# A graph-attention kernel: the scatter's one-hot made by ScalarE from a table of places instead of turned by TensorE, with a third PSUM bank for the expansion

## The reference, cut to what matters

```python
def _L0_gnn_ref(triplet_h, src, dst, Wqkv, bqkv, ...):
    h = layernorm(triplet_h, ln_attn_g, ln_attn_b)
    qkv = (h @ Wqkv + bqkv).reshape(n, 3, H, DH)
    q, k, v = qkv[:, 0] * SCALE, qkv[:, 1], qkv[:, 2]
    scores = jnp.einsum('ehd,ehd->eh', q[src], k[dst])
    m = jax.ops.segment_max(scores, dst, num_segments=n)
    e = jnp.exp(scores - m[dst])
    s = jax.ops.segment_sum(e, dst, num_segments=n)
    he = (v[src] * (e / s[dst])[:, :, None]).reshape(-1, D)
    agg = jax.ops.segment_sum(he, dst, num_segments=n)
    x = triplet_h + agg
    ...
```

## Time and profile before

| | us |
|---|---|
| median of 3 runs (3794.98 to 3800.59) | 3797.36 |
| span of the profiled execution, first to last instruction | 3773.2 |
| PE busy of it | 2896.0 (77%) |
| DVE busy | 2133.7 (57%) |
| POOL busy | 1732.1 (46%) |
| ACT busy | 963.3 (26%) |

### The profile page before, as it was taken

One profiled execution on the slowest core, in us unless ns is written; L12 is line 12 of the kernel. 1 busy time (PEld: TensorE's weight loads), 2 busy tenths in 40 slices (PEclk: granted clock), 3 DMA queues, 4 the chain that ended last, 5 costly groups with the idle time before them and its releaser, 6 DMA issues. The chain is left out here.

```text
span 3773.2 us, 52431 instructions
## 1 busy us (share of the span) xinstructions
PE 2896.0 (77%) x13207; PEld 1940.5 (51%) x13207; DVE 2133.7 (57%) x4604; ACT 963.3 (26%) x2525; POOL 1732.1 (46%) x1863
## 2 busy tenths in 40 slices
PE   6838888888888888869999999992655555555555
PEld 4525555555555555549998888871333333333332
DVE  6727776677767777768862222222544444444446
ACT  3513333333333333346663333330000000000000
POOL 2555655555555555433300000006466666666661
PEclk9968998899989999979999999995867677776678
DMA  4455666666666666533345444445233333333332
GB/s 151 147 166 164 196 192 193 181 192 189 194 188 190 192 191 195 160 114 99 99 136 210 187 186 188 187 178 164 69 91 92 92 92 92 91 91 92 92 92 88
DMA packets 233908, 557.07 MB, mean 148 GB/s; under 512 B 48498, under 2 KB 128454, under 8 KB 221095
## 3 DMA queue, kind: packets, MB, share of 16 engines
q0 software_dynamic: 104144, 324.24, 30.4%
q1 hardware_dynamic: 108463, 193.61, 14.1%
q10 hardware_dynamic: 21032, 35.85, 3.2%
HBM read 402.87 MB, written 150.71 MB: 147 GB/s over the span
## 5 line engine op out<-in xcount | busy, mean ns | idle before, releaser
L1294 POOL DMA_INDIRECT rel_rows<-msg_d,msg_i_again x783 | 743.3, 949 | 976.8 <-ACTq L1274 571.7
L1314 PE MATMUL rel_ps<-rel_rows,rel_hot 128*128 x1664 | 678.5, 538 | 525.0 <-issue 364.4
L873 POOL DMA_INDIRECT qv_rows<-qv_d,src_i x832 | 798.4, 960 | 567.6 <-PE out_ps L1155 354.2
L1314 PEld LDWEIGHTS rel_ps<-rel_rows,rel_hot 128*128 128x128 f32 x1664 | 367.1, 254 | 836.5 <-issue 806.3
L1339 DVE TENSOR_TENSOR sums_all<-sums_all,rel_ps 128x256 f32 x832 | 350.4, 421 | 630.4 <-PE rel_ps L1314 247.0
L1155 PE MATMUL out_ps<-qv_rows,hot 128*128 128x264 f32 x1664 | 635.8, 467 | 44.8 <-DVE qv_rows L950 25.0
L1031 ACT COPY at_acc<-out_ps 128x264 f32 x832 | 310.3, 380 | 726.9 <-PE out_ps L1155 581.1
L1110 PE MATMUL kx<-k,hot_t 128*128 x2496 | 398.4, 297 | 64.4 <-issue 48.4
L896 DVE TENSOR_TENSOR qv_rows<-qv_rows,kx 128x512 f32<-128x512 f32 x416 | 278.7, 679 | 204.4 <-remote 121.6
L1957 PE MATMUL up_hid_ps<-up_split,ms_hTs 128*128 128x512 f32 x1416 | 347.5, 396 | 0.0
L1110 PEld LDWEIGHTS kx<-k,hot_t 128*128 128x128 bf16 x2496 | 252.9, 105 | 175.4 <-issue 108.6
(11 more groups left out here) (213 smaller groups left out, 2883.3 us busy)
## 6 DMA issues: line engine op xcount, KB each, us to landing
msg_d<-up_x SPq DMA_DIRECT2D x33, 1024.0 KB, 3.9
msg_d<-up_gelu SPq DMA_DIRECT2D x33, 1024.0 KB, 3.8
msg_d<-up_res SPq DMA_DIRECT2D x32, 1024.0 KB, 3.8
dl_b<-dlt_d ACTq DMA_DIRECT2D x50, 512.0 KB
qv_rows<-qv_d,src_i POOLq DMA_INDIRECT x832
rel_rows<-msg_d,msg_i_again POOLq DMA_INDIRECT x783
qv_d<-qv SPq DMA_DIRECT2D x6, 1820.0 KB, 7.2
agg_d<-at_acc SPq DMA_DIRECT2D x49, 132.0 KB
```

Source lines behind the costliest of these rows:

```text
L873: nc.gpsimd.indirect_dma_start(rows[:, n % SLOTS, :], None, qv_d, bass.IndirectOffsetOnAxis(ap=src_i[:, n:n + 1], axis=0)).then_inc(got[n ...
L1294: nc.gpsimd.indirect_dma_start(rows[:, at:at + FEAT], None, table, bass.IndirectOffsetOnAxis(ap=msg_i[:, e:e + 1], axis=0)).then_inc(got[e ...
L1314: nc.tensor.matmul(sum_ps[n % BANKS][:], hot[:, n % HOTS, :], rows[:, bass.ds(at, FEAT)], start=True, stop=True).then_inc(summed, 1)
```

## The change

ACT makes `hot` itself. For each step it writes |place - number| over a row of the numbers 0 to 127 (`iota_n`) into a bf16 buffer `away`, with the place of each partition's edge as a per-partition bias; for each quad it then writes relu(1 - away) into `hot`. The places come from `late_d[0]`, loaded once into `dloc` by SP ahead of the first `dl_b`. `turn_hot`, `hot_ps` and the semaphore `turned` are gone. The freed bank is a third one for `kx`, and `hot_t` has two buffers for three. The 16 new instructions per round stand singly between ACT's old ones, except for the second quad's four, which stand together, and the copy of step 15 moves ahead of them.

```diff
-HOT_RING = 3
+HOT_RING = 2
+KX_RING = 3
...
+        away = sb(ctx, "at_away", [P, 2, QUAD, P], BF16)
-        kx = [ps(ctx, f"kx{i}", [P, BATCH, FEAT]) for i in range(2)]
-        hot_ps = ps(ctx, "hot_ps", [P, QUAD, P], BF16)
+        dloc = sb(ctx, "at_dloc_s", [P, STEPS])
+        kx = [ps(ctx, f"kx{i}", [P, BATCH, FEAT]) for i in range(KX_RING)]
...
     def on_sync(sp):
         sp.sem_inc(stored, 1)
+        sp.dma_start(dloc[:], late_d[0]).then_inc(dloc_ld, 16)
...
             if k >= HOT_RING:
-                dve.wait_ge(turned, QUADS * (k - HOT_RING + 1))
+                dve.wait_ge(kx_ok, BATCHES * (k - HOT_RING + 1))
...
-        def turned_back(k, i):
-            act.wait_ge(turned, QUADS * k + i + 1)
+        def away_from(k, i, q):
+            n = UNROLL * k + QUAD * i + q
+            last = nc.scalar.activation(away[:, i % 2, q, :], iota_n[:], ACT.Abs, scale=-1.0, bias=dloc[:, n:n + 1])
+            if q == QUAD - 1:
+                last.then_inc(away_ok, 1)
+
+        def one_hot(k, i):
+            act.wait_ge(away_ok, QUADS * k + i + 1)
             if k >= 1:
                 act.wait_ge(summed, UNROLL * (k - 1) + QUAD * (i + 1))
-            nc.scalar.copy(hot[:, QUAD * i:QUAD * (i + 1), :], hot_ps[:]).then_inc(hotf_ok, 1)
+            nc.scalar.activation(hot[:, QUAD * i:QUAD * (i + 1), :], away[:, i % 2], ACT.Relu, scale=-1.0, bias=1.0).then_inc(hotf_ok, 1)
...
             if now:
+                away_from(k - 1, 0, 0)
+                away_from(k - 1, 0, 1)
                 row_ends(k - 1)
...
                 evacuate(k - 2, banks, UNROLL - 4)
+            if now:
+                away_from(k - 1, 0, 2)
+            if before:
                 evacuate(k - 2, banks, UNROLL - 3)
             if now:
+                away_from(k - 1, 0, 3)
                 columns(k - 1)
...
             if now:
-                turned_back(k - 1, 0)
+                one_hot(k - 1, 0)
...
+            if before:
+                evacuate(k - 2, banks, UNROLL - 1)
             if now:
-                turned_back(k - 1, 1)
+                for q in range(QUAD):
+                    away_from(k - 1, 1, q)
+                one_hot(k - 1, 1)
             if further:
                 load_breaks(act, k + 1)
-            if before:
-                evacuate(k - 2, banks, UNROLL - 1)
...
                 evacuate(k - 1, banks, 0)
+                away_from(k - 1, 2, 0)
                 evacuate(k - 1, banks, 1)
+                away_from(k - 1, 2, 1)
...
                 following = banks_of(k - 1, 1)
+                away_from(k - 1, 2, 2)
                 evacuate(k - 1, banks, 3)
                 banks = following
-                turned_back(k - 1, 2)
+                away_from(k - 1, 2, 3)
+                one_hot(k - 1, 2)
                 evacuate(k - 1, banks, 4)
+                away_from(k - 1, 3, 0)
                 evacuate(k - 1, banks, 5)
-                turned_back(k - 1, 3)
+                away_from(k - 1, 3, 1)
                 following = banks_of(k - 1, 2)
                 evacuate(k - 1, banks, 6)
+                away_from(k - 1, 3, 2)
                 evacuate(k - 1, banks, 7)
+                away_from(k - 1, 3, 3)
                 banks = following
                 evacuate(k - 1, banks, 8)
                 following = banks_of(k - 1, 3)
-                for s in range(9, 12):
+                evacuate(k - 1, banks, 9)
+                one_hot(k - 1, 3)
+                for s in range(10, 12):
                     evacuate(k - 1, banks, s)
...
-            if BATCHES * k + i >= 2:
-                pe.wait_ge(prod_ok, BATCHES * k + i - 1)
+            if BATCHES * k + i >= KX_RING:
+                pe.wait_ge(prod_ok, BATCHES * k + i + 1 - KX_RING)
...
-        def turn_hot(k, i):
-            if QUADS * k + i >= 1:
-                pe.wait_ge(hotf_ok, QUADS * k + i)
...
-                turn_hot(k - 1, 0)
```

More of the change, by code:

```diff
@@ L139, in gnn_program @@
                     neg_half, src_i, end_i, tab, k3, h0_d, qv_d, key_d, tile_d, dlt_d, brk_d, hb_d, fl_d, late_d, msg_i_d, tab_d)
-            attend = attention(nc, sb, ps, sem, qv_d, agg_d, dlt_d, brk_d, fl_d, hb_d, k3, ident, ident_b, ones, part,
+            attend = attention(nc, sb, ps, sem, qv_d, agg_d, dlt_d, brk_d, fl_d, hb_d, late_d, k3, ident, ones, part, iota_n,
                                src_i, end_i, tab, got)
@@ L782, in _, with attention @@
                         last.then_inc(ends_tr, 1)
-def attention(nc, sb, ps, sem, qv_d, agg_d, dlt_d, brk_d, fl_d, hb_d, k3, ident, ident_b, ones, part,
+def attention(nc, sb, ps, sem, qv_d, agg_d, dlt_d, brk_d, fl_d, hb_d, late_d, k3, ident, ones, part, iota_n,
               src_i, end_i, tab, got):
@@ L798, in attention @@
     shift_ok, exp_ok, p_ok, resc_ok, val_ok = (sem(f"at_{n}") for n in ("shift", "exp", "p", "resc", "val"))
-    turned, hotf_ok, summed, cleared, init_ok, own = (sem(f"at_{n}") for n in ("turned", "hotf", "sum", "clear", "init", "own"))
+    away_ok, hotf_ok, summed, cleared, init_ok, own = (sem(f"at_{n}") for n in ("away", "hotf", "sum", "clear", "init", "own"))
+    dloc_ld = sem("at_dloc")
     acc_ok, acc_st, stored, turn = (sem(f"at_{n}") for n in ("acc", "accs", "stored", "turn"))
@@ L895, in product @@
             q = rows[:, slot(k, BATCH * i):slot(k, BATCH * i) + BATCH, 0:FEAT]
[L896 removed]
+            nc.vector.tensor_tensor(q, q, kx[(BATCHES * k + i) % KX_RING][:], ALU.mult).then_inc(prod_ok, 1)
         def head_sums(k, quad):
@@ L1033, in on_scalar @@
         act.wait_ge(init_ok, 1)
+        act.wait_ge(dloc_ld, 16)
         for k in range(1, ROUNDS + 2):
@@ L1119, in turn_scores @@
             nc.tensor.transpose(score_t, sc[:, k % 2], ident[:]).then_inc(st_ok, 1)
-        def turn_hot(k, i):
-            if QUADS * k + i >= 1:
-                pe.wait_ge(hotf_ok, QUADS * k + i)
-            for q in range(QUAD):
-                s = QUAD * i + q
-                last = nc.tensor.transpose(hot_ps[:, q, :], hot_t[:, k % HOT_RING, s * P:(s + 1) * P], ident_b[:])
-            last.then_inc(turned, 1)
         def turn_ends(k):
@@ L1209, in on_tensor @@
                 clear(late(14))
-            if before:
-                turn_hot(k - 1, 1)
             if old:
@@ L1217, in on_tensor @@
                 expand(k, tiles, 4)
-            if before:
-                turn_hot(k - 1, 2)
             if now:
@@ L1252, in on_tensor @@
             older_tiles, old_tiles, tiles = old_tiles, tiles, ahead
-    return Programs(on_sync, on_gpsimd, on_vector, on_scalar, on_tensor, acc_st=acc_st, places_turned=(turned, QUADS * ROUNDS))
+    return Programs(on_sync, on_gpsimd, on_vector, on_scalar, on_tensor, acc_st=acc_st, places_read=(kx_ok, BATCHES * ROUNDS))
 def edge_sum(nc, sb, ps, sem, table, sums, iota_n, late, place, msg_i, idx_ld, late_ld, x1_d, x1_all, got):
@@ L1550, in on_vector @@
                 dve.wait_ge(w_ld[0], 16)
-                dve.wait_ge(*attend.places_turned)
+                dve.wait_ge(*attend.places_read)
                 nc.vector.tensor_copy(win[:, 0], win_raw).then_inc(w_split, 1)
```

6 lines of the change are left out of this document (2 added, 4 removed).

## The result

The kernel after took 3806.64 us (median of 7 runs, 3796.55 to 3819.48), the kernel before beside it 3797.36. The ratio is 1.0029 with an interval of [1.0015, 1.0043]: slower by 0.3%, where 3726 and faster by 1.9% was forecast. The time lies in the forecast range, on the other side of no change. A second comparison, on another chip, gave 1.0035 [1.0015, 1.0056].

What follows compares the result with a forecast made beforehand. No engine full: a ring of waits between DVE, PE and ACT sets the 26.44 us round. Terms -0.4 - 1.05 - 0.35 + 0.3 + 0.1 = -1.4 us, times 52, plus 2, gave 3726 us; 8-in-10 range 3645 to 3825.

Steps and rivals of the forecast that it cites:

- Part 1: PE loses four groups of transposes a round; DVE's wait before `rescale` goes: -0.4 us a round; PE busy down 83 us.
- Part 2: ACT's copy of step 6 no longer waits behind the fourth quad's cast; all up to L910 earlier: -1.05 us a round.
- Part 3: PE's low clock after its idle stretch shortens with the shorter wait: -0.35 us a round, bounds +1.0 and -1.0.
- Part 4: ACT's 16 new instructions at 0.38 us and four relus delay `columns` by 0.3 and `row_ends` by 0.1 us a round.
- covered by DVE's own work: 0: Second quad: copy of step 0 and PE's next clear 0.9 us late, costing nothing; 0.9 to 1.4 if uncovered.
- Part 5: Third bank for the expansion and two one-hot buffers: 0 us a round, -0.2 at best.
- Part 6: One load of the places, 426 KB, ahead of the first `dl_b`: +2 us once.
- C: ACT becomes the late engine at the copy of step 0: +0.8 us a round, 3841 us; chance 0.19.
- B: PE was not on the path where shortened, ACT's +0.4 cancels the transposes' -0.4: 3799 us; chance 0.09.
- A: PE's late answers come from the transposes; the product's wait shrinks some 2 us more: -3.4 a round, 3622 us; chance 0.17.
- E: Abs and relu need other function tables than exp, two loads a round: +133 us, 3930 us; chance 0.02.
- D: PE idles more and its low clock comes once more a round, cancelling the gain: 3797 to 3799 us; chance 0.05.

Runs made afterwards that it cites:

- f1: The kernel before, unchanged, run again for a trace on one chip with f2 and f3 ("before, again"); ratio to before 1.0024, round 26.63 us.
- f2: The kernel after, unchanged, run again for a trace on the chip of f1 ("after, again"); ratio to before 1.0035, round 26.77 us.
- e3: The kernel before with one transpose of each quad's four in every round but the first, casts and waits kept; ratio to before 1.0041.
- e6: The kernel after with two banks for the expansion and sixteen unread matmuls a round where the transposes stood; ratio to before 1.0038.
- g4: The kernel before with only its fourth cast moved behind the copy of step 9; ratio to before 1.0049.
- e1: The kernel after with load_breaks, load_flags and banks_of(0) put between the second quad's four Abs and its Relu; ratio to before 0.9919.
- g1: The kernel of e1 with banks_of(0) behind the second quad's first Abs and both loads behind the copy of step 0; ratio to before 0.9925.
- f3: The kernel of e1 (loads first) run again, on the chip of f1 and f2; ratio to before 0.9946, round 26.12 us.
- g3: The kernel of e1 with four more, unread Abs beside the fourth quad's, between the copies of steps 4 to 8; ratio to before 0.9989.
- f4: The kernel of e1 with two PSUM banks for the expansion instead of three; ratio to before 0.9947.
- e8: The kernel of e1 with two banks for the expansion and the sixteen unread filling matmuls; ratio to before 1.0073, round 26.73 us.

## Why the prediction was wrong, point by point

- **Part 1, the transposes (-0.4).** The wait at `rescale` did go (35.8 us in f1, 11.8 in f2), but the time didn't: e3 and e6 put such work at nothing in these orders, with its effect on the clock in it. PE's busy time in the window fell from 1115.9 (f1) to 1090.4 us (f2), 25 and not 83 us: the transposes' own group has 81.3 us there, but its records overlap with those of the neighbours, which counts once in the union (without them it would be 1082.8 in f1, so 33 us less), and the records that stay take longer.
- **Part 2, the copy of step 6 behind the cast (-1.05).** The cast wasn't the main cause of the late copy: in g4 the copy of step 6 stands as far behind that of step 5 (4.05 us) with no cast ahead of it, though both come earlier in the round (0.82 us for step 6). The size at L910 was nearly right: 0.90 us earlier in f2, 1.27 in g4. The step that failed is that I ended the path at L910 and took what is gained there for a gain of the round. g4 has 1.27 us at L910 and 0.06 at the next exponents, and the ratio has no gain at all.
- **Part 3, the clock (-0.35).** The clock stayed at 0.90, nothing came of it. In e1 and g1, whose rounds are shorter, it was 0.94 and 0.95.
- **Part 4, ACT (+0.4).** The sizes were nearly right (401 ns for 380; the copy of step 0 0.96 us later behind the exponents, 4.70 against 3.74, where I had counted 0.9), and so was the place. The price was not: "covered by DVE's own work: 0" is the step that turned the sign. Bringing that copy forward (3.65 in f3) gains 0.66 us a round. The pieces "between copies, barely covered" cost a third of their length (g3). `columns` cost somewhat more than the +0.3: DVE's waits at its maxima, all releasers together, went from 24.0 us in f1 to 49.4 in f2, 0.5 a round. The two Abs ahead of `row_ends` cost more than the +0.1 too, if DVE's waits there (L916, L920 in after) are theirs: 10.1 became 26.9 us, 0.3 a round.
- **Part 5, the third bank (0).** Right: f3 and f4, 0.9946 and 0.9947. **Part 6 (+2 once)** fits: the first `places` comes at 227.9 us in f2 and at 224.8 in f1, though a kernel with the same load (f3) has 226.4.
- **The base.** I set 3773.2 + 24.2 against the median; the 24.2 were a quicker execution. This changed no term, since the difference was taken from the median, but by the time of `edge_sum` the rows were those of another chip than the comparison's.
- **The rivals.** C had the place and 3841; the measured 3806.6 is a fifth of the way to it from 3797.4. Its condition, that ACT isn't back in time for step 6, didn't come: in f2 that copy starts 0.11 us (median) after the end of its scatter's record. By the prediction's own numbers it couldn't with 0.45 an instruction: nine Abs of 0.07 more make the 0.9 us 1.5, not 2. B's 3799 is nearer in size, and e3 and g4 have its outcome: shortening PE's way to L910 is worth nothing. A fell: PE's late answer at step 6 did go, but the product's wait grew instead of shrinking by 2 us. E didn't come about, nor did D in after, where the clock is 0.90 as before; e3 is like it. I had given C and B 0.28 together, and the forecast 0.48 on the strength of one round's reading.

For a version that beats both kernels: the change with the loads ahead of the second Relu, at 0.992 to 0.995 in three sets, 19 to 31 us under the kernel before. That is about a third of what was forecast for the change.

## What to carry to other kernels

In a ring of waits, a shorter wait at one place is no gain of the period until it has come all the way round. Follow the forecast past the place where it is gained, up to the same mark of the next round; or move one piece alone and see whether the period moves, before adding up what each wait might give. When work goes to an idle engine, look at what it must issue around it: loads and register reads that stand behind the new work are bare time, and the same ones ahead of it are partly covered (2.48 and 1.43 us of idle time here). And take away an engine's work only after asking who will be late then: sixteen useless matmuls on TensorE cost nothing with ScalarE late, and 1.3% or more with ScalarE on time.

## What the runs showed of the hardware

- **Chips differ by up to 0.9%.** The kernel before took 3760.7 and 3764.4 us on one chip and 3788.6 to 3794.4 on three others. Profiles of before and of after from different chips can differ by more than this change does; the span of an unchanged stage (1182 against 1192 us here) gives it away.
- **PE's answers come long after the records' ends.** In before, again, ACT's copy of step 6 starts 3.68 us (median) after the end of its scatter's record, those of steps 0 to 2 and 8 after 0.11 to 0.17. With a cast moved (g4) it is 2.58 at the same step, and with three of four transposes gone (e3) 2.65. In after, again, it is 0.11 there, and the longest is 2.03 at step 13; at steps 0 and 1 (1.67 and 1.50) ACT itself is the late one. With two banks and the filler in the transposes' place (e6) it is 0.11 at step 6 too, so it isn't matmul work of that amount that makes the answer late. The cause stays open.
- **Clock and round go together; which is the cause isn't shown.** Over most of these kernels the round is 28.12 us at a clock of 0.84, 26.98 at 0.87, 26.5 to 26.8 at 0.89, and 25.7 to 26.2 at 0.93 to 0.95; e8 stands apart, with 26.73 at 0.91. Useless work that raised the clock by 0.02 (e6) won no time.
- **Issue work hides under running instructions.** `load_breaks`, `load_flags` and five registers cost 2.48 us of idle ACT behind a Relu and 1.43 with the same instructions sent during four Abs, each read in one round. Over all rounds the copy behind them starts 4.70 us after the exponents in f2 and 3.65 in f3.
